# Down product of an adaLN block: token tiles in pairs, matmuls alternating between two PSUM banks

## The reference, cut to what matters

```
mod = silu(c) @ wmod                       # sa, ca, ga, sb, cb, gb for each batch
h = layernorm(x) * (1 + ca) + sa
x = x + ga * (h @ (weight * block_mask).T)
h = layernorm(x) * (1 + cb) + sb
w1, w2, w3 = dequant_nf4(...)              # blocks of 64 with a scale each
u = silu(h @ w1.T) * (h @ w2.T)            # hidden size 2752
x = x + gb * (u @ w3.T)                    # the down product
```

## Time and profile before

| | |
|---|---|
| median of 3 runs | 1569.66 us |
| profiled execution, span from first to last instruction | 1567.6 us |
| PE busy | 1539.4 us (98%) |
| DVE busy | 1029.5 us (66%) |
| ACT busy | 989.6 us (63%) |
| DMA, mean over the span | 221 GB/s |
| matmuls | 7200, of which 1848 in the down product |

### The profile page before, as it was taken

The page is one execution under the profiler, slowest core; times in us unless marked ns, Lnnn a source line. Parts: engine busy times, 40 slices in busy tenths (PEclk is TensorE's granted clock), DMA queues, the critical chain, the costliest instruction groups (busy, mean ns, idle before and its releaser), DMA issues.

```text
span 1567.6 us, 19154 instructions
## 1 busy us (share of the span) xinstructions
PE 1539.4 (98%) x7200; PEld 1269.6 (81%) x7200; DVE 1029.5 (66%) x1486; ACT 989.6 (63%) x1290; POOL 5.5 (0%) x10
## 2 busy tenths in 40 slices
PE   5899999999999999999999999999999999999999
PEld 3688888888888888888888888888888888888887
DVE  5687786555555455547676666666875757956994
ACT  3475676998888888884898988785433432333220
POOL 0000000000000000000000000000000000000000
PEclk9999999999999999999999999999999999999999
DMA  9976423564555445532778787786777868947973
GB/s 368 372 258 228 134 81 138 177 200 166 186 169 187 153 162 180 178 128 97 257 228 252 207 250 208 207 254 171 260 292 272 332 204 302 343 160 268 397 279 122
DMA packets 170139, 345.97 MB, mean 221 GB/s; under 512 B 14752, under 2 KB 65344, under 8 KB 170048
## 3 DMA queue, kind: packets, MB, share of 16 engines
q1 hardware_dynamic: 170048, 344.76, 65.1%
HBM read 249.77 MB, written 94.93 MB: 220 GB/s over the span
## 4 chain that ended last, share of the span: by engine, by line
PE 96%; DMA 2%; DVE 0%; ACT 0%; SPq 0%; issue 0%
PE ps L1916 10%; PE ps L1915 10%; PE ps L1914 10%; PE ps L1988 9%; PE ps L1987 9%; PE ps L1989 9%; PE ps L1925 9%; PE ps L1927 9%; PE ps L1926 9%; PE ps L1832 4%; PE ps L1834 4%; PE ps L1833 4%; DMA wmod<-wmod 2%; PE ps L1789 2%; PE ps L1772 1%; DVE attn_w_lo L1368 0%
## 5 line engine op out<-in xcount | busy, mean ns | idle before, releaser
L861 ACT ACTIVATE w_raw<-w_raw 128x1024 f32<-128x1024 f32 x287 | 304.6, 1061 | 9.1
L1914 PE MATMUL ps<-ffn_in_hi,w_hi 128*128 128x512 f32 x688 | 268.6, 390 | 0.0
L1916 PE MATMUL ps<-ffn_in_hi,w_lo 128*128 128x512 f32 x688 | 267.8, 389 | 0.0
L1915 PE MATMUL ps<-ffn_in_lo,w_hi 128*128 128x512 f32 x688 | 267.7, 389 | 0.0
L1987 PE MATMUL ps<-t_hi,s_hi 128*128 128x512 f32 x616 | 239.6, 389 | 0.0
L1988 PE MATMUL ps<-t_lo,s_hi 128*128 128x512 f32 x616 | 239.6, 389 | 0.0
L1989 PE MATMUL ps<-t_hi,s_lo 128*128 128x512 f32 x616 | 239.6, 389 | 0.0
L1925 PE MATMUL ps<-x_m_hi,stream_hi 128*128 128x512 f32 x604 | 235.0, 389 | 0.0
L1926 PE MATMUL ps<-x_m_lo,stream_hi 128*128 128x512 f32 x604 | 235.0, 389 | 0.0
L1927 PE MATMUL ps<-x_m_hi,stream_lo 128*128 128x512 f32 x604 | 235.0, 389 | 0.0
L1114 ACT ACTIVATE s_hi<-s_raw 128x1408 fp32r<-128x1408 f32 x56 | 77.4, 1383 | 241.2 <-DVE s_raw L1624 192.6
(11 more groups left out here) (136 smaller groups left out, 2078.1 us busy)
## 6 DMA issues: line engine op xcount, KB each, us to landing
s_raw<-h_d SPq DMA_DIRECT2D x96, 704.0 KB, 5.6
stream_raw<-t_d SPq DMA_DIRECT2D x150, 256.0 KB, 3.4
t_d<-combined SPq DMA_DIRECT2D x106, 256.0 KB, 2.6
wmod<-wmod SPq DMA_DIRECT2D x12, 2048.0 KB, 15.3
t_raw<-w_d SPq DMA_DIRECT2D x88, 256.0 KB, 6.1
w_codes<-w12q SPq DMA_DIRECT2D x41, 512.0 KB, 5.3
h_d<-h_tile SPq DMA_DIRECT2D x44, 256.0 KB, 2.4
h_d<-up_c SPq DMA_DIRECT2D x44, 256.0 KB, 3.3
```

The source lines that it names most:

```text
L861: act.activation(RAWF[r], RAWF[r] if j else RQ[r][:], ACT.Prelu, bias=bias, scale=sign, alpha=slope).then_inc(line_ready, 1)
L1914: pe.matmul(acc, RH[r][:, k, :], HH[:, b, k, :], start=(k == 0), stop=False)
L1915: pe.matmul(acc, RH[r][:, k, :], HL[:, b, k, :], start=False, stop=False)
L1916: last = pe.matmul(acc, RL[r][:, k, :], HH[:, b, k, :], start=False, stop=(k == C - 1))
```

## The change

PE no longer finishes one tile before it begins the next. Tiles 0 to 53 go in pairs (m, m + 1): for each chunk, high by high for both tiles, then high by low for both, then low by high for both, so that two successive matmuls write different banks. All waits of both tiles (s_lo, the banks) stand ahead of the pair's first matmul. In the last chunk both tiles increment m_done, one matmul apart. The tiles 54 and 55 run one after the other, as before. ACT's copy_product and DVE's use_product move one step later in their programs, to m - 2, and DVE has one more use_product ahead of finish_last. SP's program is as it was.

```diff
--- before.py
+++ after.py
@@ -1160,8 +1160,8 @@
                 if i + 1 < len(PRODUCTS) and 1 <= j <= len(UNITS):
                     for k in UNITS[j - 1]:
                         t_high(i + 1, k)
-                if m >= 1:
-                    copy_product(m - 1)
+                if m >= 2:
+                    copy_product(m - 2)
 
         @block.vector
         def _(dve):
@@ -1743,10 +1743,11 @@
                         t_units(i + 1, UNITS[j - 1])
                     elif j == JT - 1:
                         t_low(i + 1, HC - 1)
-                if m >= 1:
-                    use_product(m - 1)
+                if m >= 2:
+                    use_product(m - 2)
                 if m + 2 < MTILES:
                     s_low(m + 2)
+            use_product(MTILES - 2)
             finish_last(MTILES - 1)
 
         @block.tensor
@@ -1965,8 +1966,8 @@
                     pe.wait_ge(tt_lo, stream_at(FULL, UP_AT[a]) + 1)
                 block_product(ps[:, tail_bank(b), :], TT[FULL % 2][UP_AT[a]], x, n % 2 == 0, n % 2 == 1)
 
-            def down_tile(m):
-                i, j, p = m // JT, m % JT, m % 4
+            def down_ready(m):
+                i, j = m // JT, m % JT
                 pe.wait_ge(s_lo, m + 1)
                 if m == 0:
                     pe.wait_ge(up_c_step, UP_STEPS * FULL)
@@ -1980,17 +1981,27 @@
                         pe.wait_ge(m_copied, m - 7)
                     else:
                         pe.wait_ge(c_step, c_ops((m - 8) // JT) + C_OPS[PRODUCTS[(m - 8) // JT][0]] * (j + 1))
-                acc = ps[:, m % 8, :]
+
+            def down_tiles(tiles):
+                i = tiles[0] // JT
+                for m in tiles:
+                    down_ready(m)
                 for k in range(HC):
-                    if j == 0:
+                    if tiles[0] % JT == 0:
                         pe.wait_ge(t_lo, i * HC + k + 1)
-                    pe.matmul(acc, SH[p][:, k, :], TH[place(i)][k][:], start=(k == 0), stop=False)
-                    pe.matmul(acc, SH[p][:, k, :], TL[place(i)][k][:], start=False, stop=False)
-                    last = pe.matmul(acc, SL[p][:, k, :], TH[place(i)][k][:], start=False, stop=(k == HC - 1))
-                last.then_inc(m_done, 1)
-
-            for m in range(MTILES):
-                down_tile(m)
+                    for m in tiles:
+                        pe.matmul(ps[:, m % 8, :], SH[m % 4][:, k, :], TH[place(i)][k][:], start=(k == 0), stop=False)
+                    for m in tiles:
+                        pe.matmul(ps[:, m % 8, :], SH[m % 4][:, k, :], TL[place(i)][k][:], start=False, stop=False)
+                    for m in tiles:
+                        last = pe.matmul(ps[:, m % 8, :], SL[m % 4][:, k, :], TH[place(i)][k][:], start=False, stop=(k == HC - 1))
+                        if k == HC - 1:
+                            last.then_inc(m_done, 1)
+
+            for m in range(0, MTILES - 2, 2):
+                down_tiles((m, m + 1))
+            for m in (MTILES - 2, MTILES - 1):
+                down_tiles((m,))
 
 
 def kernel(**inputs):
```

## The result

The changed kernel takes 1660.81 us (1660.12 to 1665.05, four runs), the kernel before 1569.54: a ratio of 1.0585, 95% interval 1.0571 to 1.0599, so 91 us more. The forecast was 1635.6 with a range to 1660, and the measured median lies 0.8 us above that range. The direction held, the size did not: 91 us where 66 were forecast.

The account below looks back on a forecast made before the run. The prediction took PE's own matmul rate, 226.7 ns each, to bound the down product. It added 58.9 us of stalls from slot turnaround and 7 us of clock loss to 1569.7, giving 1635.6 us, range 1600 to 1660.

Parts of the forecast that it names:

- The boundary rows: Trace rows where a tile ends and the bank changes: distance 0.22 us, 0.23 inside a tile, so no gain or loss taken.
- The rival at 1545: Down product: same-bank accumulation costs PE 13.4 ns per matmul and the turnaround fits in two tiles; 25 us faster, chance 0.03.
- the 18 listed: PE stalls for s_lo at the start and before 17 later pairs, 0.3 to 8.4 us each, together 58.9 us.
- the recurrence with its L: start(k) = max(end(k-1), end(k-2) + L(k)), end = start + 14.96 us; L runs from pair k-2's end to the second tile's low part.
- L by stage: Turnaround of the stationary slots reckoned per pair from landings and DVE iterations: about 12 to 25.2 us, against 14.96 available.
- 6.0 us for a double load: Stationary load of 2 x 704 KB on SP's queue: lands 6.0 us after its issue.
- a t unit 2.8 behind it: Moving-operand unit of four pieces queued behind a stationary load: 2.8 us of DMA queue at 0.38 MB/us.
- One sign: Row before the change: a t unit behind a double load landed 9.4 us after the load's issue.
- carried through the recurrence, all eight cost 13. I take half, 7: Clock loss behind the eight stalls longer than 3.2 us: 13 us for all, 7 us taken.
- one row of 1.7: Clock price per fall: after 3.20 us idle, 32 modulation matmuls took 3.62 us instead of 1.93, 1.7 us lost.
- The rival at 1659: Clock falls at nearly all gaps and stays down longer, 3 us each over ten gaps, 30 us; 1659 us, chance 0.16.
- Its upper end, 1660: Top of the range 1600 to 1660; each L 1 us longer and all stalls costing clock gave 87 us, 1657.

Follow-up runs that it names:

- pairs without preparation: Changed kernel without loads, sums, high and low parts of the stationary operands from tile 4 on; PE reuses the slots' first contents: 1573.12 us, 1.0017.
- The two halves of the cause: Changed kernel, matmuls tile after tile: with only the pair's common wait kept, 1591.23 us; with only the slots' release at the pair's end kept, 1584.50 us.
- the repaired order: Changed kernel with SP, ACT and DVE also in steps of two tiles, next pair's needs first, and stores a pair later on SP: 1582.07 us, 1.0071.
- The late stores: Changed kernel with only finish_io(m - 4) in place of finish_io(m - 2) on SP: 1658.07 us, 1.0560.
- the fillers: Changed kernel with 271 dummy matmuls ahead of 12 pairs, placed before the wait for s_lo: 1652.88 us, 1.0519.
- s_low first: Changed kernel with DVE's s_low(m + 2) directly behind s_add(m + 2), ahead of t_units and use_product: 1626.86 us, 1.0370.

## Why the prediction was right, and where it was wrong

**The matmuls: right.** Nothing gained or lost by changing banks; shown by the pairs without preparation, 226.7 ns. The boundary rows between two tiles had told it already. The rival at 1545 falls. The 216 ns of the Trainium skill (TensorE: Matmul & The Clock Gate, section Back-to-back issue gap), which that section gives for an isolated matmul, are not reached here in either order; the trace has 226.7, and that decides.

**The place of the cost: right.** All of PE's new waits are for s_lo, at the start of pairs. 14 were seen; of the 18 listed, the four missing ones (13, 15, 21, 23) were put at 0.3 to 1.8 us. As forecast every second pair is free from pair 8 on. The two halves of the cause and the repaired order show that the turnaround of the slots makes the loss.

**The size of the stalls: too small.** 58.9 forecast (the stalls as listed add up to 58.4, the recurrence with its L gives 58.8), 70.8 measured. Eleven of the 14 waits came within 2 us of the list; those of pairs 12, 14 and 22 were 2.6, 4.1 and 2.5 longer. The step that failed is "L by stage", and in it the landing times: 6.0 us for a double load, and a t unit 2.8 behind it. In pair 14 (rows above) the first t unit took 10.3 instead of 8.8. In pair 12 the double load took 8.6 instead of 6.0, and DVE's two iterations behind it 7.9 and 7.4, where 8.0 and 7.4 were reckoned. The issue, the sum that waited for the load, and DMA in that stretch (columns as in the earlier trace rows):

```profile
1344.34 1.40 SPq L635 DMA_DIRECT2D s_raw<-h_d  x2
```

```profile
1352.92 1.62 DVE L1624 TENSOR_TENSOR s_raw<-s_raw 128x1408 f32<-128x1408 f32 x1 [10.70 <-DMA s_raw<-h_d]
```

```profile
1344.30:1352.90 8.60, 8.60 (x40) 7.12 (x39) 0.00 (x0) 0.00 (x0) 0.00 (x0) 1.00 0.80 254
```

In pair 10 the slots came free at 1304.4, and the first t unit was there after 8.4 us instead of 7.0:

```profile
1312.85 0.69 DVE L1636 TENSOR_TENSOR t_raw<-t_raw 128x512 f32<-128x512 f32 x1 [10.04 <-DMA t_raw<-w_d]
```

One sign stood in the rows before: the t unit behind a double load came after 9.4 us, and the forecast went on with 6.0 + 2.8 = 8.8. The queue was reckoned at 0.38 MB/us; in the 8.6 us of pair 12 shown it moved 254 GB/s, 0.25 MB/us. Why the transfers are slower there no run shows. The late stores take SP's stand at the store away and leave the stalls, so that is not it.

**The clock: far too small, and this is the larger error.** 7 us forecast, 24.9 measured as slow matmuls; it is 18 us too small, the stalls 12. The step was "carried through the recurrence, all eight cost 13. I take half, 7". Both factors were off. The same eight waits as forecast were longer than 3.2 us, and behind all eight the clock fell (17.7 us together, by the distances between the starts behind them); it also fell behind four waits of 1.8 to 2.6 us (6.9 together). And each fall cost 1.6 to 2.7 us, where one row of 1.7 was taken for all. That row could not show more: its 32 matmuls end after 3.62 us, slow nearly throughout. The rule of the Trainium skill (TensorE: Matmul & The Clock Gate, section HAM oscillation - how this bites in real kernels), of which I had taken half, is borne out by this trace for the eight waits longer than 3.2 us, and my own price of 13 for it was low. The rival at 1659, with a chance of 0.16, comes nearest, in part by luck: it has 59 us of stalls and 30 of clock, where 71 and 25 were measured in the profiled execution.

**The range.** Its upper end, 1660, had L 1 us longer (69.9 us of stalls, which is nearly what came) and the clock at the single row's 1.7 us, 17 in all, where 25 came. The clock is what carried the time out of the range. A longer wait did not cost more of it: behind the 9.60 us of pair 14 the slow matmuls took 1.8 us, behind the 4.7 of pair 7 they took 2.7.

## What to carry to other kernels

A ring of four slots that is taken and returned in twos isn't a ring of four: the time allowed for a refill falls from three tiles for one load to two tiles for two loads. Reckon the turnaround from release to ready, along each in-order program, before grouping work on an engine that is never idle. And if that engine is TensorE, price each stall with what the clock takes behind it: here 25 us came on top of 71.

## What the runs showed of the hardware

The granted clock fell after shorter idle times than the forecast had counted with (more than 3.2 us). After 2.0 us of idle at the start of the stage it was 0.50 for the 3.4 us shown above, while after a wait of 1.11 us at 1214.0 it stayed at 1.00 in the 11 us behind.

```profile
1146.74 0.70 PE L1993 MATMUL ps<-t_hi,s_hi 128*128 128x512 f32 x2 [2.00 <-DVE s_lo L1629]
...
1214.00 0.70 PE L1993 MATMUL ps<-t_hi,s_hi 128*128 128x512 f32 x2 [1.11 <-DVE s_lo L1629]
```

In this execution 12 of the 14 waits were followed by slow matmuls; the exceptions are the one of 1.11 and one of 1.93 us. The other runs show how little a wait's length alone settles. The same wait of 2.0 us at the start of the stage was not followed by slow matmuls in the pairs without preparation (a clock of 1.00 from 1147.2 to 1151.0), with the fillers, or with s_low first. And with s_low first a wait of 3.59 us had a clock of 1.00 in the 7.8 us behind it:

```profile
1482.21 0.70 PE L1992 MATMUL ps<-t_hi,s_hi 128*128 128x512 f32 x2 [3.59 <-DVE s_lo L1629]
```

So for waits of this length a forecast of the clock has to be a chance, not a yes or no.
